# Delta heads: the second merge level of a block inverse as pairs of 32x32 products, and the key norms behind the last merge

## The reference

```python
q = _causal_conv(x @ Wq.T, cw_q, cb_q)      # k, v likewise: 4 taps, bias, silu
g = jnp.exp(-jnp.exp(A_log)[None, None, :] * jax.nn.softplus(a + dt_bias[None, None, :]))
beta = jax.nn.sigmoid(b)
q = _l2norm(q.reshape(Bb, Ss, H, DK))       # k likewise
def step(Sstate, inputs):
    q_t, k_t, v_t, g_t, beta_t = inputs
    retrieved = jnp.einsum('bhkv,bhk->bhv', Sstate, k_t)
    error = v_t - g_t[..., None] * retrieved
    update = k_t[..., :, None] * (beta_t[..., None] * error)[..., None, :]
    Snew = g_t[..., None, None] * Sstate + update
    o_t = jnp.einsum('bhkv,bhk->bhv', Snew, q_t)
    return (Snew, o_t)
```

## Time and profile before

| | |
|---|---|
| runs, median (n = 3) | 3424.02 us |
| profiled execution, its own time | 3412.34 us |
| its span | 3410.5 us |
| busy PE | 3186.3 us (93%) |
| busy PE weight loads | 2542.9 us (75%) |
| busy DVE | 2190.4 us (64%) |
| busy ACT | 1900.5 us (56%) |
| busy POOL | 1675.2 us (49%) |
| `delta_heads`, its 64 slots | about 155 to 1706 us of the span |
| PE busy in that stretch of 1551.00 us | 1528.02 us |
| one head, slots c=1, 2, 3 and the next c=0 | 25.17, 25.26, 25.10, 23.91 us |

### The profile page before, as it was taken

The page is one execution under the profiler, slowest core; times in us unless marked ns, Lnnn a source line. Parts: engine busy times, 40 slices in busy tenths (PEclk is TensorE's granted clock), DMA queues, the critical chain, the costliest instruction groups (busy, mean ns, idle before and its releaser), DMA issues. The chain is left out here.

```text
span 3410.5 us, 60026 instructions
## 1 busy us (share of the span) xinstructions
PE 3186.3 (93%) x18834; PEld 2542.9 (75%) x18834; DVE 2190.4 (64%) x4849; ACT 1900.5 (56%) x4657; POOL 1675.2 (49%) x3107
## 2 busy tenths in 40 slices
PE   6899999999999999999999788799979999998998
PEld 3688888888888888888878555488866776776543
DVE  5577777677777767777653588665547567575432
ACT  3677777777777777777532377644446445463111
POOL 2777787778778777778530000145534002021322
PEclk8899999999999999999999899899989999999999
DMA  4222222222222222222363333423351111211843
GB/s 117 60 73 69 60 69 63 78 63 72 69 60 68 63 78 62 72 69 60 91 182 86 115 142 142 177 86 103 114 170 62 68 69 69 93 63 49 277 96 59
DMA packets 432408, 310.47 MB, mean 91 GB/s; under 512 B 130496, under 2 KB 347456, under 8 KB 431072
## 3 DMA queue, kind: packets, MB, share of 16 engines
q1 hardware_dynamic: 423792, 289.57, 28.6%
q0 software_dynamic: 8432, 18.88, 2.7%
HBM read 177.97 MB, written 130.43 MB: 90 GB/s over the span
## 5 line engine op out<-in xcount | busy, mean ns | idle before, releaser
L631 PE MATMUL gd_PJ<-xn_lead,gd_w_rest 128*128 128x512 f32 x1024 | 421.6, 412 | 0.5 <-DVE gd_w_rest L786 0.5
L631 PE MATMUL gd_PJ<-xn_lead,gd_w_lead 128*128 128x512 f32 x1024 | 403.2, 394 | 0.0
L631 PE MATMUL gd_PJ<-xn_rest,gd_w_lead 128*128 128x512 f32 x1024 | 402.0, 393 | 0.0
L1079 POOL TENSOR_TENSOR gd_prod<-gd_L,gd_T 32x14 f32<-32x14 f32 (+6 forms) x896 | 323.0, 361 | 70.7
L1082 POOL TENSOR_TENSOR gd_T<-gd_T,gd_prod 32x14 f32<-32x14 f32 (+6 forms) x896 | 315.3, 352 | 71.7 <-POOL gd_prod L1079 2.7
L793 DVE SCALAR_TENSOR_TENSOR gd_conv<-gd_pre,gd_cur_a,gd_conv 128x512 f32<-128x512 f32 x384 | 301.4, 785 | 13.3 <-ACT gd_conv L958 3.0
L631 PEld LDWEIGHTS gd_PJ<-xn_lead,gd_w_lead 128*128 128x128 f32 x1024 | 193.9, 189 | 43.6
L631 PEld LDWEIGHTS gd_PJ<-xn_lead,gd_w_rest 128*128 128x128 f32 x1024 | 194.5, 190 | 38.5 <-DVE gd_w_rest L786 0.9
L631 PEld LDWEIGHTS gd_PJ<-xn_rest,gd_w_lead 128*128 128x128 f32 x1024 | 194.8, 190 | 35.3
L2619 ACT ACTIVATE sa_E<-sa_B,sa_nmax 128x512 f32<-128x512 f32 (+3 forms) x256 | 131.6, 526 | 131.9 <-DVE sa_nmax L2756 131.9
L932 DVE SCALAR_TENSOR_TENSOR gd_og<-gd_B,ptab,gd_gate 128x512 f32<-128x512 f32 x64 | 48.1, 751 | 243.6 <-PE gd_B L645 243.6
(11 more groups left out here) (476 smaller groups left out, 8680.3 us busy)
## 6 DMA issues: line engine op xcount, KB each, us to landing
expert_rows<-xt_blank SPq DMA_DIRECT2D x16, 2112.0 KB, 7.3
turned_queries_keys<-f_wq SPq DMA_DIRECT2D x16, 1280.0 KB, 6.0
x_wo<-decay_sums SPq DMA_DIRECT2D x64, 256.0 KB, 3.7
triangles<-gd_Lo SPq DMA_DIRECT2D x64, 256.0 KB, 3.4
gd_W<-turned_image SPq DMA_DIRECT2D x64, 256.0 KB, 2.9
gd_T<-inverse_image SPq DMA_DIRECT2D x64, 256.0 KB, 3.3
gated_outputs<-gd_og SPq DMA_DIRECT2D x64, 256.0 KB, 2.8
go_ogt<-gated_outputs SPq DMA_DIRECT2D x16, 1024.0 KB, 6.0
```

The lines of the kernel that those rows point to most:

```text
L631: mm = pe.matmul(bank, w_parts[wp][:, j, k, :], rhs, start=(k == 0 and wp == 1), stop=(k == KT - 1 and wp + xp == 0))
L1079: nc.gpsimd.tensor_tensor(prod[:, rows, 0:j], L16[:, rows, j:j + 1].to_broadcast(shape), T16[:, j:j + 1, 0:j].to_broadcast(shape), ALU.mul ...
```

## The change

Level 1 is computed on the two 64-row halves of the matrix (q = 0 and q = 64) apart, each as products of 32x32: `spread_rows(1)` and `merge(1)` are now eight small products each instead of four of 128x64, in banks `half[2]`, `half[3]` and free columns of bank 0. The transposed blocks go to a tile `inv` instead of back into `T`, so two small transposes (64x4x64 and 32x4x32) replace the one of 128x512. masked(1) and merged(1) become two operations of 32x4x32 each, and the corner is transposed straight from PSUM. The order on DVE changes: turned_blocks stands ahead of key tap 2; merged(1) and turned_corner right behind masked(1), ahead of query tap 0 and the JK weights; masked(2) behind query tap 0; kdiag and the key sum behind the query taps; merged(2) ahead of the key norm chain. On ACT the Sqrt moves from ahead of oi to behind the silu of the queries. PE counts a new semaphore, `blocks_open`, twice a slot, and waits for `og_ready` of the slot before spread_rows(1).

```diff
@@ -463,6 +463,7 @@
         T = sb("T", [P, 2, B, P])
         W = sb("W", [P, 2, B, P])
         Y = sb("Y", [P, 2, B, P // 2])
+        inv = sb("inv", [P, B, TOP + TOP // 2])
         PT = sb("PT", [P, B, P])
         Kd = sb("Kd", [P, B, P])
         Vb = sb("Vb", [P, B, P])
@@ -486,6 +487,9 @@
         PJ = ctx.enter_context(nc.psum_tensor("gd_PJ", [P, 2, BN], F32))
         Bk = [ctx.enter_context(nc.psum_tensor(f"gd_B{k}", [P, B, P], F32)) for k in range(6)]
         half = [Bk[k][:, 0:2, :].rearrange("p a (h c) -> p (a h) c", h=2) for k in range(6)]
+        SIDE = MERGE[1]
+        PAIRS = ((0, half[2]), (2 * SIDE, Bk[0][:, :, 0:SIDE]))
+        UPPERS = ((0, half[3]), (2 * SIDE, Bk[0][:, :, SIDE:2 * SIDE]))
 
         cst_in, w_in, image_in, wo_in = sem("cst_in"), sem("w_in"), sem("image_in"), sem("wo_in")
         og_out = [sem("og_out0"), sem("og_out1")]
@@ -503,7 +507,7 @@
         kdiag, k_len, q_len, k_root, k_max, k_rnorm, q_max, q_rnorm, once_ready, scales_done, extra_done = (
             sem(x) for x in ("kdiag", "klen", "qlen", "kroot", "kmax", "krnorm", "qmax", "qrnorm", "once", "scales", "extra"))
         solving, solved, cleared, masks_set = sem("solving"), sem("solved"), sem("cleared"), sem("masks_set")
-        y_sum, y_ready, wup, w_ready, t_next = (sem(x) for x in ("ysum", "y", "wup", "w", "t"))
+        y_sum, y_ready, wup, w_ready, inv_ready, blocks_open = (sem(x) for x in ("ysum", "y", "wup", "w", "inv", "blocks"))
         ks_done, r_ready, oi_sum, oi_ready, u_sum, u_ready, o_sum, o_ready, s_sum, s_ready, sd_ready = (
             sem(x) for x in ("ks", "r", "oisum", "oi", "usum", "u", "osum", "o", "ssum", "s", "sd"))
         og_ready, o2_ready, osq_done = sem("og"), sem("o2"), sem("osq")
@@ -661,8 +665,16 @@
                         pe.wait_ge(o_ready, n + 1)
                     else:
                         pe.wait_ge(w_ready, n * NM + l)
-                    if l < NM - 1:
+                    if l == 0:
                         each(half[2], tiles(Lo_c), [second(W_c, MERGE[l])[:, b] for b in range(B)], y_sum)
+                    elif l == 1:
+                        pe.wait_ge(og_ready, n + 1)
+                        pe.sem_inc(blocks_open, 1)
+                        for b in range(B):
+                            for q, bank in PAIRS:
+                                lo, hi = slice(q, q + SIDE), slice(q + SIDE, q + 2 * SIDE)
+                                mm = pe.matmul(bank[lo, b, 0:SIDE], Lo_c[hi, b, lo], W_c[hi, b, hi], start=True, stop=True)
+                        mm.then_inc(y_sum, 1)
                     else:
                         each(half[2][0:TOP], [Lo_c[:, b, 0:TOP] for b in range(B)], [W_c[:, b, TOP:P] for b in range(B)], y_sum)
 
@@ -670,12 +682,18 @@
                     pe.wait_ge(y_ready, n * NM + l + 1)
                     if l == 0:
                         pe.wait_ge(p_ready, n + 1)
+                        each(half[3], tiles(T_c), [Y[:, l % 2, b, :] for b in range(B)], wup)
+                        return
+                    pe.wait_ge(inv_ready, n * (NM - 1) + l)
+                    if l == 1:
+                        pe.sem_inc(blocks_open, 1)
+                        for b in range(B):
+                            for q, bank in UPPERS:
+                                at = slice(q, q + SIDE)
+                                mm = pe.matmul(bank[at, b, 0:SIDE], inv[at, b, q:q + SIDE], Y[at, l % 2, b, 0:SIDE], start=True, stop=True)
+                        mm.then_inc(wup, 1)
                     else:
-                        pe.wait_ge(t_next, n * (NM - 1) + l)
-                    if l < NM - 1:
-                        each(half[3], tiles(T_c), [Y[:, l % 2, b, :] for b in range(B)], wup)
-                    else:
-                        each(half[3][0:TOP], [T_c[:, b, 0:TOP] for b in range(B)], [Y[:, l % 2, b, :] for b in range(B)], wup)
+                        each(half[3][0:TOP], [inv[:, b, 0:TOP] for b in range(B)], [Y[:, l % 2, b, :] for b in range(B)], wup)
 
                 if back and more and c == CH - 1:
                     pe.wait_ge(g_silu, n + 2)
@@ -805,6 +823,12 @@
                     if l == NM - 1:
                         nc.vector.tensor_scalar(Y[0:TOP, l % 2], half[2][0:TOP], -1.0, None, ALU.mult).then_inc(y_ready, 1)
                         return
+                    if l == 1:
+                        for q, bank in PAIRS:
+                            at = slice(q, q + SIDE)
+                            ts = nc.vector.tensor_scalar(Y[at, l % 2, :, 0:SIDE], bank[at, :, 0:SIDE], -1.0, None, ALU.mult)
+                        ts.then_inc(y_ready, 1)
+                        return
                     nc.vector.tensor_tensor(Y[:, l % 2], half[2], levels[:, 64 * l:64 * l + 64].unsqueeze(1).to_broadcast([P, B, P // 2]),
                                             ALU.mult).then_inc(y_ready, 1)
 
@@ -814,17 +838,22 @@
                     if l == NM - 1:
                         nc.vector.tensor_copy(W_c[0:TOP, :, TOP:P], half[3][0:TOP]).then_inc(w_ready, 1)
                         return
+                    if l == 1:
+                        for q, bank in UPPERS:
+                            tc = nc.vector.tensor_copy(W_c[q:q + SIDE, :, q + SIDE:q + 2 * SIDE], bank[q:q + SIDE, :, 0:SIDE])
+                        tc.then_inc(w_ready, 1)
+                        return
                     nc.vector.tensor_tensor(second(W_c, s), second(W_c, s), half[3].rearrange("p b (g m) -> p b g m", m=s),
                                             ALU.add).then_inc(w_ready, 1)
 
                 def turned_blocks():
                     dve.wait_ge(w_ready, n * NM + 1)
-                    nc.vector.transpose(T_c, W_c).then_inc(t_next, 1)
+                    nc.vector.transpose(inv[0:TOP, :, 0:TOP], W_c[0:TOP, :, 0:TOP])
+                    at = slice(2 * SIDE, 3 * SIDE)
+                    nc.vector.transpose(inv[at, :, at], W_c[at, :, at]).then_inc(inv_ready, 1)
 
                 def turned_corner():
-                    s = MERGE[1]
-                    dve.wait_ge(w_ready, n * NM + 2)
-                    nc.vector.transpose(T_c[s:2 * s, :, 0:s], W_c[0:s, :, s:2 * s]).then_inc(t_next, 1)
+                    nc.vector.transpose(inv[SIDE:2 * SIDE, :, 0:SIDE], half[3][0:SIDE, :, 0:SIDE]).then_inc(inv_ready, 1)
 
                 if back:
                     masked(0)
@@ -838,6 +867,7 @@
                     tap(n + 2, par, PK, cur_k, (1,), k_tap)
                 if back:
                     merged(0)
+                    turned_blocks()
                 if has2:
                     tap(n + 2, par, PK, cur_k, (2,), k_tap)
                 if not back and c == 2:
@@ -850,27 +880,26 @@
                                                             in1=Vb[:, b, :], op0=ALU.mult, op1=ALU.add)
                     st.then_inc(r_ready, 1)
                 if back:
-                    turned_blocks()
                     masked(1)
+                    merged(1)
+                    turned_corner()
                 if has1:
                     dve.wait_ge(q_halo, n + 2)
                     dve.wait_ge(q_pre, n + 2)
                     tap(n + 1, parm, PQ, cur_a, (0,), q_tap)
                 if back and more and c == 1:
                     rest_weights(i + 1, JK)
+                if back:
+                    masked(2)
+                if has1:
+                    tap(n + 1, parm, PQ, cur_a, (1, 2), q_tap)
                 if has2:
                     dve.wait_ge(kk_done, n + 3)
                     nc.vector.tensor_tensor(diag[:], Bk[4][:, :, :], ident.unsqueeze(1).to_broadcast([P, B, P]), ALU.mult).then_inc(kdiag, 1)
-                if back:
-                    merged(1)
-                if has2:
                     dve.wait_ge(kdiag, n + 3)
                     nc.vector.tensor_reduce(kss[:, :], diag[:], AX.X, ALU.add).then_inc(k_len, 1)
                 if back:
-                    turned_corner()
-                    masked(2)
-                if has1:
-                    tap(n + 1, parm, PQ, cur_a, (1, 2), q_tap)
+                    merged(2)
                 if has2:
                     dve.wait_ge(k_root, n + 3)
                     nc.vector.tensor_scalar(klen[:, :], klen[:, :], 1e-12, None, ALU.max).then_inc(k_max, 1)
@@ -884,9 +913,6 @@
                     nc.vector.tensor_tensor(once[:, par], both, by, ALU.mult).then_inc(once_ready, 1)
                     dve.wait_ge(once_ready, n + 3)
                     nc.vector.tensor_tensor(twice[:, par], once[:, par], by, ALU.mult).then_inc(scales_done, 1)
-                if back:
-                    merged(2)
-                if has2:
                     dve.wait_ge(scales_done, n + 3)
                     dve.wait_ge(d_exp, n + 3)
                     for b in range(B):
@@ -934,6 +960,7 @@
                                                    in1=gate[:, par, :], op0=ALU.mult, op1=ALU.mult).then_inc(og_ready, 1)
 
```

(7 more changed lines are left out.)

## The result

The changed kernel took 3431.11 us as the median of 20 runs, the kernel before 3420.03 us in 20: slower, ratio 1.0032, interval 1.0024 to 1.0040, some 11 us. The forecast was +14 us and 3438; the time, the sign and the range were right. The profile says that a good part of the reasoning was not. The profiled execution of the changed kernel took 3435.29 us (span 3433.5), the one of before 3412.34. These two are 23 us apart, twice as far as the medians, so the profiles show where time goes, and the medians how much. Of the 23 us, 14.4 lie in the 14 heads in the middle (a head is 99.47 us before and 100.50 after, in the mean) and some 7 in the last head.

The account below looks back on a forecast made before the run. The prediction took a head-long loop through PE, DVE, POOL and DMA as the bound. +0.25 (c=1), 0 (c=2) and +0.69 (c=3) gave +0.94 us a head, +14 us over 15 heads on 3424.02: 3438 us, range 3416 to 3462.

Parts of the forecast that it names:

- The sum: Per head, c=1 +0.25, c=2 0 and c=3 +0.69 give +0.94 us; over 15 heads +14 us.
- segment two: PE's first product of c=1 to the query-norm clamp in c=3, 68.99 us; only gains here count.
- segment one: Query-norm clamp in c=3 through POOL and DMA to PE's next c=1, 30.45 us; claimed untouched by the change.
- The loop: Head-long 99.44 us loop through PE, DVE, POOL and DMA; PE's gains in c=3's rest and c=0 only lengthen its wait.
- the third sign: The prediction counts as wrong if `Lo` in c=3 isn't later.
- Narrow groups: Level-1 groups on PE: 0.76 us each, 0.08 less than now, from 0.23 form change and 16 pairs at 0.033.
- Rival B: Level-1 pairs on PE are cheap: at 0.025 a group is 0.63 us, total +3 to +6 us; chance 0.21.
- c=1, +0.25: Slot c=1: projection V waits for the JK weights' rest, now behind merged(1) on DVE; +0.25 us a head.
- c=2, 0: Slot c=2: transposes delay key tap 2 by some 0.54 us, yet merge(1) hardly moves; counted 0, ends -0.1 and +0.1.
- c=3, +0.69: Slot c=3: the key norm chain now stands between merged(2) and `Lo`, making `Lo` and the clamp 0.69 us later.
- Rival C: POOL's solve in c=0: DVE's new pattern spares two long operations a head, shortening it; -10 us, 3414; chance 0.14.

Follow-up runs that it names:

- e2: The changed kernel with ACT's copy of the next head's first K moved ahead of the squares of o: 3430.61 us, ratio 1.0038 to the kernel before.
- e7: The changed kernel with the two small transposes moved behind key tap 2, just ahead of masked(1): 3419.27 us, ratio 1.0014 to the kernel before.
- e4: The kernel before with only the changed kernel's order on DVE and ACT, products left wide: 3427.76 us, ratio 1.0026 to the kernel before.
- e6: The changed kernel with the rest of the JK weights in c=1 moved ahead of query tap 0: 3434.77 us, ratio 1.0052 to the kernel before.
- e8: The changed kernel with transposes and key norms moved back, next head's K copy ahead of the squares, JK rest ahead of query tap 0: 3426.93 us, ratio 1.0035.
- e12: e7 plus e2's and e6's edits, and in c=3 the key norm chain and `Lo` behind the query-norm clamp: 3396.36 us, ratio 0.9943 to the kernel before.
- e9: e7 with ACT's two exponentials moved ahead of the values' silu: 3436.94 us, ratio 1.0054 to the kernel before.
- e10: e9 with the next head's K copy ahead of the squares and the JK rest ahead of query tap 0: 3432.0 us, ratio 1.0047.
- e11: The kernel before with only ACT's two exponentials moved ahead of the values' silu: 3441.25 us, ratio 1.0068.

## Why the prediction was right, and where it was wrong

**The number.** +11 us measured, +14 forecast, and that it came so close is luck. The sum put +0.94 us a head into segment two and nothing into segment one. In the profiles, by the means of 14 heads, segment two grew by 0.43 (69.02 to 69.45) and segment one by 0.60 (30.45 to 31.05), and what lengthened segment one, the clock falls, stood in none of my cases. So the number is no evidence for the terms of the sum.

**The loop: right for the kernel before, but closed too early.** "What PE gains in the rest of c=3 and in c=0 makes it wait longer for the same DMA" held only while the DMA was last. e2 and e7 show that loop coming back when c=0 is short. In the changed kernel itself two things moved. POOL's solve in c=0 took 15.0 us instead of 16.3, and PE came later. So segment one, which "the change touches no instruction of", changed length: 29.8 us in the head without a clock fall (clamp 1027.60 to PE's 1057.38), 32.1 in one with it (1227.56 to 1259.64), 30.45 before. Its end is now PE's own work in c=0 and not the DMA. PE's wait for `gd_T` in c=1, which was to grow to 1.4 to 2.0 us, went away. So what was to show the prediction wrong, "if segment one moves by over 0.3 us", did happen, and "if a group's step is outside 0.63 to 1.21" as well; only the third sign, a `Lo` that isn't later, did not. Nor did the new order do away with PE's wait for merged(1) in c=0: it was 0.63 and is 0.68 (0.51 in e4, with wide groups).

**Narrow groups: mis-sized.** 0.37 us, 0.47 with the entry, for my 0.76. Of the fixed costs the entry came out near mine (0.10 for 0.08), the exit lies within the 0.37 and can't be told apart; the spacing of 0.033 was 0.015, outside the ends that I had kept. Rival B had the sign of this right and its size too small, and the mechanism that it names, two row groups that alternate, would fit the loads that come in twos; no run here takes the alternation away.

**c=1, +0.25.** The mechanism was there: PE stood for the JK rest in each head, 0.73 us in the mean. But projection V began no later than before, 10.77 us after the head's first product for 10.75, so the term was +0.02: what the cheap groups saved on PE and in the chain to merged(1) made up for it. In e4, with wide groups, it began 0.61 us later. e6 shows that the wait was worth nothing by itself. My own sum had a slip of 0.06 here: merge(1) at 958.65, a group of 0.76 and 0.20 give 959.61 and not 959.55.

**c=2, 0: right for the slot, wrong for the transposes.** The slot itself got no longer (25.51 us for 25.64). But the transposes ahead of key tap 2 are the dearest single place that a run took back (e7). The rows are DVE in the same slot c=1 as above:

```profile
1061.85 0.44 DVE L851 STREAM_TRANSPOSE gd_inv<-gd_W 64x256 f32<-64x256 f32 x1
1062.31 0.30 DVE L853 STREAM_TRANSPOSE gd_inv<-gd_W 32x128 f32<-32x128 f32 x1
1062.64 0.75 DVE L811 SCALAR_TENSOR_TENSOR gd_conv<-gd_pre,gd_cur_k,gd_conv 128x512 f32<-128x512 f32 x1
```

They delay the tap by 0.79 us, where I had 0.54. And I compared kT's delay with an arrival of PE after an almost unchanged group. With a group of 0.37 PE came early and the delay showed, in c=2 and above all in c=0, which I had not looked at for kT, since c=0 counted for nothing.

**c=3, +0.69.** The chain did go between merged(2) and `Lo`, and the clamp came 0.54 us later in the slot in the mean. What I missed is the second way on from it: values' silu, exponentials, gate, squares, K copy, key taps, kT of the next head. PE ended c=3 0.64 us earlier, and against that the K copy in c=0 was 1.2 us late and the transposes came on top of it.

**Rival C** (POOL's operations come in two lengths, and DVE's pattern decides) did happen: its price, two spared operations a head or 1.6 us, was right, by the solve's length in c=0 (16.3 us to 14.7 in the mean of 14 heads). But it was spent where the solve no longer bounds. e4, the order alone, has the solve at 15.1, and e8, with the transposes and the key norms moved back, at 16.3 again, so its length goes with the order on DVE and ACT. Whether the two engines wait for each other at the memory, as rival C had it, was not tested. B's price for the pairs happened as well, and more than that; it did not make the kernel equal, since the gain went into waits.

**The clock** was in none of my cases. The rows of before had 1.00 in all 14 heads, and I took it as given, while the change made PE stand in c=0 for 1.33 to 1.61 us and again for 0.68.

## What to carry to other kernels

Where one engine is 98% busy and waits once a period for a loop through other engines, write down every segment of the period with what ends it, and ask of each saved us who stands still for it. If the saving engine is TensorE, the standing itself can cost: in this kernel useless matmuls in a gap took the clock falls out of slot c=0 in 15 heads. Edits that gain nothing alone (e2 and e6 brought nothing) can still be part of a version that gains: e12 has them together with e7 and with a release of POOL that comes earlier, ahead of a chain and a triangle that nobody waits for yet. Which of the three did it was not measured. And before slots of two kernels are compared, they have to be cut at the same event on the same engine: cut at DVE's `og`, the start of c=1 lies 0.22 us ahead of PE's first product before, and 0.44 behind it after, and the changed kernel's c=0 looks longer and its c=1 shorter than they are.

## What was not expected of the hardware

- Weight loads of 32x32 followed one another every 0.015 us in the mean (16 in 0.33 us), where the lowest spacing of before was 0.025.
- The granted clock fell from 1.00 to about 0.54 for some 7 us after PE had been busy for 2.17 of 3.50 us, in a kernel whose PE is otherwise busy nearly all the time; with the gap filled it did not fall. The same waits did not always bring it on: with 1.33 to 1.58 and 0.68 us it stayed at 1.00 in four heads of the changed kernel, with up to 0.96 and 0.52 in all heads of e4, but with 0.61 and 0.68 it fell in one head of e7.
- POOL's turn of the head took 2.5 to 2.9 us in all runs but e12 (2.8 to 3.2), also in e9, e10 and e11, where ACT's exponentials were done 2.5 us or more before its end.
